# Second attention of a sandwich block: the first query tile's scores in two products and two blocks

## The reference, cut to what matters

```python
x = rmsnorm(hidden_states, ln1_w)
q, k, v = ...                       # 16 heads of 128 columns each
scores = einsum('bqnd,bknd->bnqk', q, k) * 192 ** -0.5
scores = where(causal, scores, -1e9)
p = softmax(scores)
attn = einsum('bnqk,bknd->bqnd', p, v)
attn_out = einsum('bsd,hd->bsh', attn, o_w)
```

## Time and profile before

| what | value |
|---|---|
| median of three runs | 1232.38 us (1231.99 to 1232.53) |
| span of the profiled execution | 1230.1 us |
| TensorE busy / weight loads busy | 1172.6 us (95%) / 1004.9 us (82%) |
| VectorE / ScalarE / GpSimd busy | 859.6 us (70%) / 794.0 us (65%) / 580.0 us (47%) |
| score matmuls (L1479, `qk`, all four widths) | 768, 129.4 us |
| mask and maximum (L1114, both attentions) | 512, 235.4 us |
| granted TensorE clock | 9 tenths or more of full speed in 39 of 40 slices, 8 in the other |

### The profile page before, as it was taken

One profiled execution on the slowest core, in us unless ns is written; L12 is line 12 of the kernel. 1 busy time (PEld: TensorE's weight loads), 2 busy tenths in 40 slices (PEclk: granted clock), 3 DMA queues, 4 the chain that ended last, 5 costly groups with the idle time before them and its releaser, 6 DMA issues.

```text
span 1230.1 us, 25177 instructions
## 1 busy us (share of the span) xinstructions
PE 1172.6 (95%) x7996; PEld 1004.9 (82%) x7996; DVE 859.6 (70%) x2663; ACT 794.0 (65%) x1973; POOL 580.0 (47%) x844
## 2 busy tenths in 40 slices
PE   6999999899999999999999999999998889999986
PEld 5766566689999999999989999989996769999962
DVE  5788888576677667876677876678866755555535
ACT  3587888677777676677776677766776534444422
POOL 3063655454334444447343356434363446666650
PEclk9999999999999999999999999999999989999998
DMA  7965565256531211213111132111214247777766
GB/s 258 291 192 173 167 178 176 88 159 203 175 112 57 89 52 57 80 53 121 36 56 49 36 104 70 49 56 35 70 62 136 69 114 119 118 119 117 118 114 215
DMA packets 111780, 139.59 MB, mean 113 GB/s; under 512 B 11364, under 2 KB 94820, under 8 KB 111524
## 3 DMA queue, kind: packets, MB, share of 16 engines
q1 hardware_dynamic: 97204, 119.10, 31.9%
q0 software_dynamic: 14448, 18.88, 9.6%
HBM read 63.36 MB, written 61.87 MB: 102 GB/s over the span
## 4 chain that ended last, share of the span: by engine, by line
PE 69%; DVE 13%; ACT 8%; issue 4%; POOL 2%; DMA 2%; SPq 1%; ACTq 0%; POOLq 0%
PE bank L1479 49%; PE bank L1898 5%; PE bank L1721 5%; DVE bank L1114 3%; PE bank L1540 2%; PE bank L1576 2%; PE bank L1593 2%; ACT p L953 2%; DVE hs L1337 2%; DVE pT L1324 1%; PE bank L1877 1%; POOL xs_rows L680 1%; PE bank L1908 1%; PE bank L1583 1%; DVE qk L1213 1%
## 5 line engine op out<-in xcount | busy, mean ns | idle before, releaser
L1114 DVE CUSTOM_DVE_ANT_0 bank<-bank,mask 128x512 f32<-128x512 f32 (+3 forms) x512 | 235.4, 524 | 32.6 <-PE bank L1576 19.8
L944 ACT ACTIVATE p<-bank,stat 128x512 f32<-128x512 f32 (+3 forms) x256 | 131.5, 526 | 132.4 <-DVE stat L1114 132.4
L533 POOL CAST w_hl<-raw_qkv 128x512 fp32r<-128x512 f32 x96 | 58.7, 611 | 312.3 <-DMA raw_qkv<-in_qkvo 159.6
L1479 PE MATMUL bank<-xT,w_hl 128*128 128x512 f32 x768 | 189.2, 395 | 0.0
L1479 PEld LDWEIGHTS bank<-xT,w_hl 128*128 128x128 f32 x768 | 144.3, 188 | 33.9
L742 POOL DMA_INDIRECT sum_rows<-mid,goal x79 | 122.8, 1555 | 70.8 <-DVE mid L1443 67.0
L1479 PE MATMUL bank<-pT,v 128*128 128x128 f32 (+3 forms) x768 | 137.1, 327 | 0.0
L953 ACT ACTIVATE p<-p,stat 128x512 f32<-128x512 f32 (+3 forms) x256 | 123.1, 553 | 14.7 <-DVE stat L1340 14.7
L1479 PE MATMUL bank<-qk 128*128 128x512 f32 (+3 forms) x768 | 129.4, 317 | 3.1 <-DVE pT L1324 2.4
L1479 PEld LDWEIGHTS bank<-qk 128*128 128x128 f32 x768 | 119.3, 189 | 12.0 <-DVE v L1213 2.6
L534 POOL TENSOR_TENSOR w_hl<-raw_qkv,w_hl 128x512 fp32r<-128x512 f32 x96 | 124.2, 1293 | 7.8
(11 more groups left out here) (237 smaller groups left out, 2396.8 us busy)
## 6 DMA issues: line engine op xcount, KB each, us to landing
raw_qkv<-in_qkvo SPq DMA_DIRECT2D x32, 768.0 KB, 5.6
xs_rows<-blank SPq DMA_DIRECT2D x32, 520.0 KB, 3.5
xs_rows<-blank SPq DMA_DIRECT2D x5, 2730.0 KB, 14.1
xrow<-xs_rows SPq DMA_DIRECT2D x79, 130.0 KB, 2.5
raw_o<-in_qkvo SPq DMA_DIRECT2D x32, 256.0 KB, 3.8
sum_rows<-blank SPq DMA_DIRECT2D x3, 2176.0 KB, 9.2
stk<-xT SPq DMA_DIRECT2D x96, 64.0 KB
stk<-k_hl SPq DMA_DIRECT2D x96, 64.0 KB
```

The lines of the kernel that those rows point to most:

```text
L944: act.activation(p2[:, n % 2, POFF[qi]:POFF[qi + 1]], s2(t), ACT.Exp, scale=-1.0, bias=stat2[:, 0, n % 2, t:t + 1], accum_out=stat2[:, 1, ...
L1114: return dve.tensor_tensor_reduce(scores, scores, mask[:, TB - scores.shape[1]:], scale=-1.0, scalar=-2.0 * MASKED, op0=ALU.add, op1=ALU.m ...
L1479: ins = pe.matmul(out, a, b, start=start and i == 0, stop=stop and i == len(pairs) - 1, **kw)
```

## The change

The first query tile (t = 3, qi = 0) gets its scores from two matmuls in place of three. The first has q HI as its weights and moves 256 columns, 128 of k HI and 128 of k LO, into two neighbouring blocks of the bank. The second has q LO as its weights, moves the 128 columns of k HI, and adds to the first block. VectorE then adds the second block to the mask, into an SBUF tile `rest` (the front of `gated`, which the shared expert uses later), waits for this by `link`, and runs the same custom instruction as before with `rest` in place of the mask. The other three query tiles are as they were.

```diff
@@ VectorE
             y_stats(B - 1)
+            rest = gated[:, 0, 0:P]
...
                 if here:
                     for t in range(TPB):
                         dve.wait_ge(b_s, n * TPB + (t + 1))
-                        mask_and_max(s2(t), stat2[:, 0, n % 2, t:t + 1]).then_inc(b_max, 1)
+                        if t == TPB - 1:
+                            link(dve.tensor_tensor(rest, bank[t][:, P:2 * P], mask[:, TB - P:], ALU.add))
+                            dve.tensor_tensor_reduce(s2(t), s2(t), rest, scale=-1.0, scalar=-2.0 * MASKED, op0=ALU.add,
+                                                     op1=ALU.min, accum_out=stat2[:, 0, n % 2, t:t + 1]).then_inc(b_max, 1)
+                        else:
+                            mask_and_max(s2(t), stat2[:, 0, n % 2, t:t + 1]).then_inc(b_max, 1)
@@ TensorE, scores(t)
-                    product(s2(t),
-                            [(qk2[:, 0, s, P * qi:P * (qi + 1)], qk2[:, 1, m, 0:P * (qi + 1)])
-                             for s, m in PARTS]).then_inc(b_s, 1)
+                    if qi == 0:
+                        pe.matmul(bank[t][:, 0:2 * P], qk2[:, 0, HI, 0:P], qk2[:, 1, :, 0:P], start=True, stop=False,
+                                  skip_group_check=True)
+                        pe.matmul(s2(t), qk2[:, 0, LO, 0:P], qk2[:, 1, HI, 0:P], start=False, stop=True,
+                                  skip_group_check=True).then_inc(b_s, 1)
+                    else:
+                        product(s2(t),
+                                [(qk2[:, 0, s, P * qi:P * (qi + 1)], qk2[:, 1, m, 0:P * (qi + 1)])
+                                 for s, m in PARTS]).then_inc(b_s, 1)
```

## The result

The changed kernel takes 1238.86 us (median of eight runs, 1237.35 to 1241.06), the kernel before 1232.18 us beside it on the same chip (median of eight). The ratio is 1.0062, with a 95% interval of 1.0048 to 1.0076: slower by about 7 us, where no change to be seen was forecast (1233.2 us), and above the range of 1230.8 to 1236.9.

What follows compares the result with a forecast made beforehand. TensorE was taken to bound the kernel, almost without waits; costs of 3.2, 1.3 and 0.2 us less a gain of 3.85 gave +0.8 us, 1230.9 profiled and 1233.2 us as median, range 1230.8 to 1236.9.

Steps and rivals of the forecast that it cites:

- g: TensorE's saving per step from the two score matmuls replacing three: 0.107 us, bounds 0 to 0.107.
- The rival by which only columns count: TensorE pays per column, so the score matmuls save nothing: +4.7 us, 1237.1 us; chance 0.06.
- d: Delay on VectorE of all behind the new addition and its link: 0.32 us, bounds 0.20 to 0.45.
- Who waits for it: Step following VectorE's delay through reciprocal and ScalarE: exponential not late, ScalarE's scalings and next q and k d later.
- The remaining 36 periods gain g: Periods between scores of successive heads with enough room: each gains 0.107 us, -3.85 us in all.
- nine without room: Three periods after the squares and six with a wait for xT's LO part: each pays 0.32 us in full.
- twelve after `POST_ROW`: Periods at n = 28 to 31, 44 to 47, 60 to 63: each pays 0.11 us, +1.3 us.
- n = 12, 20, 36, 52: Four steps with little room, three of them behind a late step: +0.2 us for all four.
- n = 1 and 2: Reciprocal there waits for the exponential, which isn't late, with no residual additions ahead: cost 0.
- the room of 0.21 of the twelve, and of 0.26 of the four: Slack before TensorE must wait for q's LO part, from gaps of 0.32 (n = 28 to 31) and 0.37 (n = 12).
- the 0.11 us, taken from n = 19: Time from q's LO part done to TensorE's start at which a wait takes hold; room is the gap less this.
- The six waits for xT: TensorE's waits for VectorE's LO part of xT before a `project_v`: to grow from 0.3 to about 0.7 us.

Runs made afterwards that it cites:

- the first experiment: Changed kernel with TensorE's two products kept but VectorE leaving the HI by LO block out of the scores: 1227.81 us, ratio 0.9974 to the kernel before.
- VectorE alone: Kernel before with its three products, VectorE also forming and awaiting `rest` but then using the mask: 1241.21 us, ratio 1.0080.
- residual addition first: Changed kernel with VectorE's first residual addition moved between the new addition and the custom instruction: 1233.42 us, ratio 1.0018 to the kernel before.
- addition early: Changed kernel with the new addition moved ahead of the third tile's maximum: 1231.20 us, ratio 0.9994 to the kernel before.
- the addition twice: Changed kernel with VectorE's new addition done twice, the first copy unused: 1251.18 us, ratio 1.0162 to the kernel before.

## Why the prediction was wrong, point by point

**TensorE's saving was right.** g was put at 0.107 us, and the plain step of the first experiment is 0.10 shorter. The rival by which only columns count is refuted. The two-block matmul took 0.12 us, as the 256-wide one of the earlier trace rows, so its two pieces cost nothing. The rule of the isolated gap in the Trainium skill ("TensorE: Matmul & The Clock Gate", Back-to-back issue gap) gives a saving of under 0.003 us a step; as a price for this stream the trace does not agree with it, since the saving is 0.10.

**VectorE's delay was close.** d was put at 0.32 and is 0.28: the addition takes 0.28 and the link 0.03, as in the earlier trace rows, but the custom instruction behind a wait is 0.30 long where it was 0.33. It is 0.30 with the bfloat16 mask too (VectorE alone), so the operand has nothing to do with it.

**The step that failed is "Who waits for it".** It named the residual additions as queued behind the new work, and then followed only what lies behind them, the reciprocal and ScalarE. It did not ask who waits for the residual additions themselves. That is TensorE: the q projection of the next head waits for the bank that the first one reads. "The remaining 36 periods gain g" needed that wait among its conditions. Its room is 0.25 us, and d + g = 0.39 is over it, so TensorE stalls for 0.14 and a plain step pays 0.03 to 0.04 and does not gain 0.10.

By period, from the traces of both kernels, first scores to last:

| periods | forecast | measured |
|---|---|---|
| nine without room | +2.9 | +2.5 |
| twelve after `POST_ROW` | +1.3 | +2.3 |
| n = 12, 20, 36, 52 | +0.2 | +0.8 |
| n = 1 and 2 | 0 | +0.7 |
| the 36 that were to gain | -3.9 | +0.4 |
| sum | +0.5 | +6.6 |

Of the 36, the seven into n = 3, 4, 13, 14, 23, 39 and 55 did gain, 0.8 us together. TensorE has an extra job between the scores and the projection there, and the addition is in time. The other 29 cost 1.2 us, where 3.1 were to be gained: 4.3 us of error, out of 6.1. With the residual addition first the 36 gain 3.5 us.

**A second term was mis-sized: the room of 0.21 of the twelve, and of 0.26 of the four.** The wait for the residual addition is not the reason. The table gives what the periods into n = 28 to 31 lost (+) or gained (-) against the kernel before, as the mean of the three groups of four, beside the delay of the reciprocal in a plain step:

| kernel | delay, us | n = 28, 29, 30, 31, us | sum |
|---|---|---|---|
| changed | 0.28 | +0.20, +0.08, +0.39, +0.09 | +0.76 |
| addition first | 0.22 | +0.15, +0.03, +0.34, +0.03 | +0.56 |
| addition early | 0.15 | +0.07, -0.04, +0.26, -0.04 | +0.26 |

In all three the sum is four delays less 0.32 to 0.36, so the mean room is 0.08 to 0.09 us, also where the residual addition is on time. Only n = 29 and 31 have about the room of 0.21. What the reading of the earlier trace rows missed is seen in two places. The lateness is handed on: at n = 29 VectorE starts its first maximum 556.29 - 555.18 = 1.11 us after the scores, and 392.18 - 391.29 = 0.89 in a plain step. The rows of the changed kernel:

```profile
555.18 1.04 PE L1485 MATMUL bank<-qk 128*128 128x512 f32 x4
```

```profile
556.29 0.69 DVE L1114 CUSTOM_DVE_ANT_0 bank<-bank,mask 128x512 f32<-128x512 f32 x1
```

And the 0.11 us, taken from n = 19, does not hold for every step. At n = 30 with the residual addition first TensorE visibly stands still, and starts 561.33 - (560.38 + 0.69) = 0.26 us after q's LO part is done:

```profile
560.38 1.29 DVE L1213 SCALAR_TENSOR_TENSOR qk<-bank,qk 128x512 fp32r<-128x512 f32 x2 [0.83 <-ACT qk L886]
```

```profile
561.33 1.42 PE L1493 MATMUL bank<-wo_hl,o 128*128 128x256 f32 x10 [0.18 <-issue]
```

With 0.26 the gap of 0.32 leaves 0.06 of room, and the period into n = 28 behaves so (0.28 - 0.20 = 0.08, 0.22 - 0.15 = 0.07). The one into n = 12 has a room of 0.13 in the same way, not 0.26. Why the distance differs from that at n = 19 is open.

**What held up.** The six waits for xT grew as forecast, and the periods after the squares did, by 0.25 to 0.28. Over the three kernels of the table the nine periods without room cost 2.5, 2.0 and 1.3 us, which is nine times the delay within 0.1.

**The 0.7 us in n = 2 are the clock, not the change's work.** The period is 12.1 us and not 11.4 in the changed kernel, 12.1 with TensorE's part alone and 12.3 with the addition twice; in the other kernels it is 11.40 to 11.42. In exactly these three traces the granted clock falls to half, the level of 1.2 GHz, for 3.4 us in this stretch (from 251.7 to 255.1 in the changed kernel). Windows of 2 us, start and end, length, busy time of the engines, granted clock, DMA share, GB/s, changed kernel and kernel before:

```profile
252.00:254.00 2.00, 2.00 (x11) 2.00 (x9) 1.86 (x6) 1.07 (x3) 2.00 (x5) 0.50 0.00 0
```

```profile
252.00:254.00 2.00, 2.00 (x17) 2.00 (x17) 1.76 (x8) 1.35 (x5) 1.96 (x4) 1.00 0.00 0
```

From 248 to 251 us TensorE was busy for 0.52 us in the changed kernel and for 0.63 in the kernel before, where the clock did not fall. What decides it is not shown. A slice of the page is 31 us long, and so short a fall does not show in it. (The page of the kernel before has 8 tenths in two slices and not in one; both lie behind 980 us, outside the second attention.) Without this the periods cost +5.9 us, still far from +0.5.

## What to carry to other kernels

For work put on an in-order engine, go through everything queued behind it, and ask of each piece who waits for it, not only who waits for the last one: here a plain addition, out of the chain that I followed, held the bank of the next product. Room read off one step need not hold for another: measure it where it is used, and look whether a late step hands its lateness on. A total that comes out as expected does not confirm the sum behind it; the terms have to be read one by one. An engine that is always busy in the profile can still have little room on each of several waits, and the room is used up from both sides, by what makes the other engine late and by what makes this one early. And where the room differs from step to step, a change can be applied in the steps that have it.

## What the runs showed of the hardware

- A wait ahead of a matmul has to be met well before the matmul's turn. In the changed kernel the weight load started 0.12 us after the end of the addition that TensorE waited for, and the twelve matmuls then took 2.88 us and not 2.79. Of TensorE's 0.49 us behind that addition in the kernel before, only 0.25 were room.
- A stall of that size stands in no wait row of TensorE's matmuls, and as plain TensorE work in the chain of a plain step. What gives it away is the idle time ahead of the weight load (0.31 us, "issue"). At 0.20 us more it appears in the chain, and then as 0.09.
- TensorE's granted clock fell to half for 3.4 us near 250 us in three of the nine traces, after about the same idle time as in those where it stayed, and cost 0.7 us in a step of 11.4.
- A moving operand in two pieces of 128 columns goes at the pace of one of 256: 0.12 us.
